# A fused attention and slot-mixing kernel: TensorE's step regrouped, split products together and the plain fp32 work in one block behind them

## The reference

```python
h = layernorm(x)                                   # block 1: windowed attention over ctx
score = einsum('nqh,hk,nlk->nql', h, W_a, ctx)     # masked outside a window around p
align = softmax(score) * gauss                     # per row
x = x + tanh(concat([einsum('nql,nlh->nqh', align, ctx), h]) @ W_c.T)

h = layernorm(x)                                   # block 2: 64 slots, top 8 of them per row
logits = (gelu(concat([h, slot_mean]) @ w1 + b1, approximate=False) @ w2 + b2) / (abs(tau) + 0.1)
alpha = one_hot(top_k(logits, 8)) weighted by their softmax
slot_input = einsum('bts,btd->bsd', alpha, h); si = slot_input / (alpha.sum(axis=1) + 1e-8)
S_new = GRU(si, slots)                             # Wih, Whh, 512 x 1536 each
y = layernorm(S_new + attention(S_new)) * ln_g + ln_b     # over the 64 slots of a batch
x = x + einsum('bts,bsd->btd', alpha, y @ wvp + bvp) @ wo + bo
```

## Time and profile before

| | |
|---|---|
| time, median of 3 runs | 366.73 us (365.95 to 368.85) |
| the profiled execution, its span | 365.68 us, 363.8 us |
| PE busy | 346.7 us, 95% of the span |
| DVE, ACT, POOL busy | 253.0, 186.8, 188.9 us |
| granted TensorE clock, mean | 0.994 of full speed |
| chain that ended last | PE 71%, DVE 11%, POOL 6%, issue 4%, ACT 3%, DMA 3% |
| costliest lines of that chain | L345, L346, L347 (the split products) 12%, 11%, 11%; L1398 9%; L1448 (slot sums) 5% |

### The profile page before, as it was taken

The page is one execution under the profiler, slowest core; times in us unless marked ns, Lnnn a source line. Parts: engine busy times, 40 slices in busy tenths (PEclk is TensorE's granted clock), DMA queues, the critical chain, the costliest instruction groups (busy, mean ns, idle before and its releaser), DMA issues.

```text
span 363.8 us, 6883 instructions
## 1 busy us (share of the span) xinstructions
PE 346.7 (95%) x2246; PEld 273.4 (75%) x2246; DVE 253.0 (70%) x729; ACT 186.8 (51%) x384; POOL 188.9 (52%) x340
## 2 busy tenths in 40 slices
PE   5899999999999999999999999999999999999991
PEld 2376558899997988988898898977556597676671
DVE  0838987777788788687787787666584344768774
ACT  1261033667749568577577587478262126422341
POOL 1317055879676966776686677541011112342693
PEclk9999999999999999999999999999999999999997
DMA  5889956332323232322323100039300000002399
GB/s 167 280 278 373 394 173 170 112 114 62 115 75 103 61 115 59 103 73 62 114 60 109 38 2 2 2 74 364 119 3 0 0 2 0 3 0 86 146 346 347
DMA packets 41366, 42.78 MB, mean 118 GB/s; under 512 B 3678, under 2 KB 32478, under 8 KB 41331
## 3 DMA queue, kind: packets, MB, share of 16 engines
q1 hardware_dynamic: 39376, 40.42, 33.5%
q10 hardware_dynamic: 1666, 1.27, 1.3%
q0 software_dynamic: 288, 0.66, 0.6%
HBM read 32.18 MB, written 8.39 MB: 112 GB/s over the span
## 4 chain that ended last, share of the span: by engine, by line
PE 71%; DVE 11%; POOL 6%; issue 4%; ACT 3%; DMA 3%; SPq 0%; DVEq 0%; POOLq 0%; ACTq 0%
PE psum L345 12%; PE psum L346 11%; PE psum L347 11%; PE psum L1398 9%; PE psum L1448 5%; PE psum L1668 3%; PE psum L1294 3%; PE psum L1476 3%; DMA WvpT<-in_WvpT 2%; PE psum L1336 2%; PE psum L1692 2%; PE psum L1429 2%; PE psum L1594 2%; POOL X L491 2%; PE psum L1511 1%
## 5 line engine op out<-in xcount | busy, mean ns | idle before, releaser
L345 PE MATMUL psum<-GW_hi,hT_hi 128*128 128x292 f32 (+1 forms) x256 | 79.0, 308 | 1.1 <-POOL GW_lo L473 1.0
L347 PE MATMUL psum<-GW_lo,hT_hi 128*128 128x292 f32 (+1 forms) x256 | 74.0, 289 | 0.0
L346 PE MATMUL psum<-GW_hi,hT_lo 128*128 128x292 f32 (+1 forms) x256 | 73.9, 289 | 0.0
L491 POOL TENSOR_TENSOR X<-X,th 128x512 f32<-128x512 f32 x32 | 38.3, 1196 | 31.4 <-ACT th L1097 31.4
L345 PEld LDWEIGHTS psum<-GW_hi,hT_hi 128*128 128x128 f32 x256 | 48.4, 189 | 2.9 <-issue 2.0
L486 POOL TENSOR_TENSOR hT_lo<-xT,hT_hi 128x512 fp32r<-128x512 f32 x32 | 43.4, 1356 | 13.3 <-ACT hT_hi L1053 13.3
L346 PEld LDWEIGHTS psum<-GW_hi,hT_lo 128*128 128x128 f32 x256 | 48.3, 189 | 0.2 <-issue 0.2
L347 PEld LDWEIGHTS psum<-GW_lo,hT_hi 128*128 128x128 f32 x256 | 48.1, 188 | 0.0
L345 PE MATMUL psum<-xhT_hi,w_hi 128*128 128x256 f32 x128 | 38.4, 300 | 0.1
L346 PE MATMUL psum<-xhT_hi,w_lo 128*128 128x256 f32 x128 | 36.1, 282 | 0.0
L347 PE MATMUL psum<-xhT_lo,w_hi 128*128 128x256 f32 x128 | 36.0, 281 | 0.0
(11 more groups left out here) (261 smaller groups left out, 822.9 us busy)
## 6 DMA issues: line engine op xcount, KB each, us to landing
X<-in_x SPq DMA_DIRECT2D x32, 256.0 KB, 3.5
xT<-in_xT SPq DMA_DIRECT2D x32, 256.0 KB, 2.8
out<-ost SPq DMA_DIRECT2D x32, 256.0 KB, 2.5
WhhT<-in_WhhT SPq DMA_DIRECT2D x1, 3072.0 KB, 12.3
WihT<-in_WihT SPq DMA_DIRECT2D x4, 768.0 KB, 8.4
WvpT<-in_WvpT SPq DMA_DIRECT2D x4, 256.0 KB, 5.6
Wo<-in_wo ACTq DMA_DIRECT2D x4, 256.0 KB, 3.6
WaT<-in_WaT SPq DMA_DIRECT2D x1, 1024.0 KB
```

The costliest lines, as they stand in the source:

```text
L345: pe.matmul(out, w_hi, m_hi, start=start, stop=False)
L346: pe.matmul(out, w_lo, m_hi, start=False, stop=False)
L347: return pe.matmul(out, w_hi, m_lo, start=False, stop=stop)
L491: pool.tensor_tensor(tile_x(r), tile_x(r), halves(th[:, :]), ALU.add).then_inc(S("x2"), 1)
```

## The change

Four edits, three in TensorE's program and one in VectorE's:

- From step 3 on (`TURN_AT_END`), the softmax weights of tile s are turned at the end of step s, behind `turn_rows`, and no longer in step s + 1 between `score` and `right_half`.
- `slot_sums` moves from in front of `first_layer` to behind it, in steps 12 to 30; step 31 keeps its place.
- With it VectorE's `slot_inputs(b)` for b = 0 to 3 moves from its step 15, 19, 23, 27, where it stood ahead of the third part of the top-8 work, to the start of the next step, ahead of `low_xh`.
- `if live(s)` is dropped where it is always true, and two added lines shift all later line numbers by two (from TensorE's step on by five).

```diff
--- before.py
+++ after.py
@@ -47,6 +47,8 @@
 
 
 BIAS_STEP, GATES_STEP = 1, 1
+
+TURN_AT_END = 3
 
 EB = NB - 2
 EP, EN, LN = EB // 2, EB * NS, (NB - EB) * NS
@@ -817,6 +819,9 @@
                             ALU.subtract, ALU.mult).then_inc(S("sin"), 1)
 
         def step(s):
+            for b in range(NB):
+                if SLOT_STEP[b] + TPB == s:
+                    slot_inputs(b)
             if live(s - 3):
                 low_xh(s - 3)
             if live(s):
@@ -831,7 +836,7 @@
                 for part in range(3):
                     if TOPK_STEP[b] + part == s:
                         topk(b, part)
-                if SLOT_STEP[b] + TPB - 1 == s:
+                if SLOT_STEP[b] + TPB - 1 == s == NT - 1:
                     slot_inputs(b)
             if live(s - 1) and s < NT - 1:
                 stats2(s - 1)
@@ -1512,21 +1517,24 @@
                                  stop=True, skip_group_check=True)
             last.then_inc(S("cx"), 1)
 
-        def step(s):
-            if live(s):
-                score(s)
-            if live(s - 1):
-                turn_weights(s - 1)
-            if live(s):
-                right_half(s)
-            if live(s) and s:
-                context(s - 1)
-            if s in TOPK_STEP:
-                turn_logits(TOPK_STEP.index(s))
+        def sums_of(s):
             for b in range(NB):
                 q = s - SLOT_STEP[b]
                 if live(q, 0, TPB):
                     slot_sums(b, q)
+
+        def step(s):
+
+            score(s)
+            if live(s - 1, 0, TURN_AT_END):
+                turn_weights(s - 1)
+            right_half(s)
+            if s:
+                context(s - 1)
+            if s in TOPK_STEP:
+                turn_logits(TOPK_STEP.index(s))
+            if s == NT - 1:
+                sums_of(s)
 
             turns = [b for b in range(NB) if s == SLOT_STEP[b] + TPB or (b % 2 and s == SLOT_STEP[b] + 1)]
             if turns:
@@ -1538,6 +1546,8 @@
                     turn_alpha(b, trX, b)
             first_layer(s, 0)
             first_layer(s, 1)
+            if s < NT - 1:
+                sums_of(s)
             for b in range(NB):
                 if LOGIT_STEP[b] == s:
                     logits(b)
@@ -1545,12 +1555,13 @@
             if live(s - 2):
                 turn_rows(s - 2, len([b for b in range(NB) if SLOT_STEP[b] + TPB <= s]),
                           len([b for b in range(1, NB, 2) if SLOT_STEP[b] + 1 <= s]))
+            if s >= TURN_AT_END:
+                turn_weights(s)
 
         pe.wait_ge(S("split"), 3)
         for s in range(NT):
             step(s)
 
-        turn_weights(31)
         context(31)
         slot_sums(5, 0)
         pe.wait_ge(S("th"), NT - 1)
```

## The result

The changed kernel takes 368.89 us (median of 20 runs, 368.10 to 370.25), the kernel before 366.64 in runs beside it (20, 365.28 to 368.85): ratio 1.0067, interval 1.0054 to 1.0081, so 2.5 us slower, 2.0 to 3.0. Forecast were 369.5 and +2.8.

The account below looks back on a forecast made before the run. TensorE was taken to bound the loop; 0.4 lost in step 12 plus 2.6 in steps 16, 20, 24 and 28, less 0.3 gained, gave +2.8 us on 366.7: 369.5, range 365.6 to 371.2.

Parts of the forecast that it names:

- The bound: In the loop's body TensorE is busy 168.46 of 170 us; its time shows unless it waits for another engine.
- What a switch costs: On TensorE: slot sums alone 0.78 us, joined to logits 0.43; a turned weight tile about 0.11 wherever it stands.
- The rival that put 0.06 more on each: Turned weight tile at the block's end costs its upper bound, 28 times 0.06, 1.6 us: 371.1; chance 0.08.
- Step 12: first_layer waits for VectorE's low_xh, sums and turned weights come behind it: step ends 0.43 us later.
- VectorE's chain: Ahead of step 16's turned slots, a top-8 product waits for GpSimd, 1.48 us not 0.42; low_xh ends 0.60 later.
- Step 16: TensorE's turned slots wait for VectorE; step ends 0.66 us later; four such steps cost 2.6.
- no further wait: At turn_rows in step 16, ScalarE's copy of the turned slots ends at 144.49, ahead of 144.60: no wait.
- The sum: Whole kernel: 0.4 + 2.6 - 0.3 = +2.8 us, median 369.5, 0.8% slower.
- what the slot sums hid: In steps 12, 16, 20, 24, 28 first_layer needs VectorE's late low_xh; before, the slot sums filled that time.
- the regrouping pays in full: Rival: TensorE's joined blocks save all 2.3 us, 364.4, with low_xh early enough in five steps; chance 0.12.

Follow-up runs that it names:

- e9: Changed kernel with GpSimd's low_x behind scales2 in steps 11, 15, 19, 23, 27 and ScalarE's turned-slots copy ahead of high_x: 364.94 us, ratio 0.9952 to before.
- e1: Changed kernel with the softmax weights turned in the old place, sums and slot_inputs still moved: 369.81 us, ratio 1.0090 to the kernel before.
- e2: Kernel before with only the softmax weights turned at the end of the tile's own step: 367.27 us, ratio 1.0016.
- e5: Changed kernel with GpSimd's low_x behind scales2 in steps 15, 19, 23 and 27: 365.34 us, ratio 0.9983 to the kernel before.
- e10: Kernel before with VectorE's slot_inputs moved and GpSimd's low_x behind scales2 in steps 15, 19, 23 and 27: 366.24 us, ratio 1.0008.
- e3: Kernel before with only VectorE's slot_inputs moved to the start of the next step, ahead of low_xh: 369.83 us, ratio 1.0095.
- e4: Changed kernel with the slot sums in front of first_layer again in steps 12, 16, 20, 24 and 28: 368.69 us, ratio 1.0070 to the kernel before.
- e6: Kernel before with logits directly behind slot sums, ahead of first_layer, every fourth step from 12; some sums later, slots' copy earlier: 364.74 us, ratio 0.9944.

## Why the prediction was right

- **The bound.** TensorE bounds the loop and other engines' lateness shows only where it waits: borne out. It did the same work in 3.3 us more.
- **What a switch costs.** A pair of records in mid-block at 0.215, so sums joined to logits 0.43 more: 0.44 in step 12, and 0.44 in step 16 of e9; 0.46 in step 16 of the changed kernel, where the slots' copy ends just ahead of the turned rows. A turned tile at 0.11 in the block: 0.24 from 119.10 to 119.34, less 0.13 for a plain product of 292 columns, is 0.11. The rival that put 0.06 more on each falls, by e1 and e2 too. Steps 13 to 15, 21 and 29 are 0.05 to 0.08 shorter; I took 0.05 for the sums ahead of the turned rows. The sums alone save 0.03 to 0.07 there (e1), and the moved tile alone 0.01 to 0.03 (e2), for which I took nothing. In steps 17 and 25, which turn `alpha`, nothing is saved, which the sum had wrong by 0.05 each.
- **Step 12**: +0.43 forecast, +0.43 measured, by the wait forecast.
- **VectorE's chain**: 1.48 for the top-8 product forecast and measured, `low_xh` 0.60 later forecast and, counted from the start of step 14, 0.64 measured. The shared port pair's lock of the Trainium skill (SBUF — State Buffer, "SBUF: two separate sides") is what the trace shows in steps 15, 19, 23 and 27, and e5 and e10 show the neighbour to be the cause: without it 0.42.
- **Step 16**: from the start of step 14 to its end +0.66 forecast, +0.71 measured. Steps 20, 24 and 28 came out at +0.91, +0.77 and +0.76 counted alike, 3.15 in all for the 2.64 forecast. The term that was too small, by 0.5 in all, is mainly the wait for ScalarE's copy of the turned slots. I had its end 0.11 ahead of the turned rows and said "no further wait". But where TensorE waits for the copy it starts the rows 0.15 behind its end in step 16 and some 0.25 behind it in the others (e2, e3, e4), and the kernel before already stood there, 0.16 behind it and 0.26 to 0.27 in steps 20, 24 and 28. So there was nothing to spare. In the changed kernel it is 0.15, 0.41, 0.25 and 0.24; in step 20 the profile puts 0.22 of idle time down to no engine, and some 0.16 of that stays unexplained. With the slots' copy ahead of `high_x` (e9) all four steps take 7.09, where e5 took 7.12 in step 16 and 7.23 or 7.24 in the others. A smaller part: from the turned slots to the second product of `first_layer` it took 0.39, where I had taken 0.35.
- **The sum**: +2.8 forecast; +2.5 by the ratio, +3.0 to +3.2 like with like, +3.3 by the loop. So the forecast was 0.2 to 0.5 too small. That the ratio puts it 0.3 too large instead is luck: the median of the kernel before lies in its longer group, that of the changed kernel in its shorter one.
- **What it left out**: the sums of a new batch wait for `slot_inputs` of the old one (`sin`). In the changed kernel that wait never binds, since the sums come late; it is why "what the slot sums hid" was the right story for step 12 and only half of it for the other four. There VectorE's order alone costs 2.7 with the sums in their old place. Rival "the regrouping pays in full" needed just what e9 supplies, and got 1.8 of its 2.3 us.

## What to carry to other kernels

Joining work of one kind into a block pays what the trace's start distances say, here 0.30 us for each pair of fp32 blocks where 0.35 was summed (e6, steps 12 and 16), and it pays only where the place that the work leaves doesn't turn into a wait. Before moving work on the bounding engine, ask what that work was covering and how near the next wait stands, and move the block to the cover, not the cover to the block. And a small operation moved on a side engine can cost most of its length (here 0.61 to 0.67 a step for the 0.82 of `slot_inputs`) when it had run in the time that its neighbour on GpSimd blocks anyway.

## What the runs showed of the hardware

- A VectorE tensor-tensor operation that starts 0.1 us behind a GpSimd one of 1.3 us took 1.48 us for its own 0.42, in ten of ten such places (steps 11, 15, 19, 23 and 27 of the changed kernel and of e3). One that starts 0.1 us ahead took 0.42 to 0.45, and GpSimd's operation 1.36 for its usual 1.19. The one that came second ended 0.27 to 0.29 behind the first in all ten.
- A block of plain fp32 products on 64 columns of the array took 0.58, 1.01 and 1.45 us for two, four and six pairs of records: about 0.215 per pair and 0.15 for the block. Between a split product and the block 0.10 more passed on the way in. A turned fp32 tile of 128 columns took 0.11 between split products and 0.11 at the end of the block.
- I had not expected how even the rest is: steps 2 to 6 agree to 0.03 us each over the twelve traces, although five of these kernels turn a tile elsewhere from step 3 on (the preparation ahead of the loop does not: its end varies by 1.0 us).
